# A two-layer perceiver kernel: input rows loaded alone, weight loads moved into the first chunks, the causal convolution's SiLU moved beside the x products

## What is computed

```
x = x + xattn0(layernorm(x), ctx, ctx)     # 8192 units: gelu(x @ ctx.T) @ ctx
x = x + mamba(layernorm(x), ...)           # W_in -> x_inner, z; causal conv of 4 taps;
                                           # silu; W_x; W_dt; selective scan; * silu(z); W_out
x = x + ffn0(layernorm(x), w1, w2)         # quantised weights and activations
x = x + xattn1(ctx, layernorm(x), ...)     # attention over 8192 + 512 keys
x = x + attn1(layernorm(x), ...)           # attention over channels
x = x + moe(layernorm(x), ...)             # 8 experts, top 2, and a shared one
```

## Time and profile before

| | |
|---|---|
| median of 3 runs | 2829.2 us (2828.49 to 2832.64) |
| the profiled execution, its own time | 2823.83 us |
| its span | 2822.1 us |
| TensorE matmul busy | 2561.9 us (91%) |
| VectorE busy | 1889.8 us (67%) |
| ScalarE busy | 1108.7 us (39%) |
| GpSimd busy | 529.2 us (19%) |
| mean granted TensorE clock | 0.954 of full |

### The profile page before, as it was taken

The page is one execution under the profiler, slowest core; times in us unless marked ns, Lnnn a source line. Parts: engine busy times, 40 slices in busy tenths (PEclk is TensorE's granted clock), DMA queues, the critical chain, the costliest instruction groups (busy, mean ns, idle before and its releaser), DMA issues.

```text
span 2822.1 us, 33960 instructions
## 1 busy us (share of the span) xinstructions
PE 2561.9 (91%) x11618; PEld 1674.2 (59%) x11618; DVE 1889.8 (67%) x2048; ACT 1108.7 (39%) x1340; POOL 529.2 (19%) x381
## 2 busy tenths in 40 slices
PE   6999988866755799999989999999989799999999
PEld 5778877622222566666654444444467677777775
DVE  5887853199988667777786666666545566666664
ACT  2333422333335322222215555555433355555553
POOL 4555542056630221111110000000010100000000
PEclk9999999999986899999989999999989899999999
DMA  7667745700010233343421232223111356666663
GB/s 281 234 237 253 259 132 164 268 8 15 23 60 1 94 134 146 124 173 119 163 90 61 90 124 100 90 90 125 40 45 45 123 206 223 225 225 223 224 224 131
DMA packets 105450, 394.40 MB, mean 140 GB/s; under 512 B 22842, under 2 KB 23046, under 8 KB 73108
## 3 DMA queue, kind: packets, MB, share of 16 engines
q1 hardware_dynamic: 77380, 326.61, 31.6%
q10 hardware_dynamic: 27984, 66.66, 6.7%
HBM read 303.93 MB, written 89.30 MB: 139 GB/s over the span
## 4 chain that ended last, share of the span: by engine, by line
PE 64%; DVE 11%; issue 3%; ACT 1%; POOL 1%; DMA 0%; DVEq 0%; SPq 0%; ACTq 0%; POOLq 0%
PE ps L1971 13%; PE ps L1973 12%; PE ps L1972 12%; PE ps L2269 10%; PE ps L2278 9%; DVE ps L1502 5%; PE ps L2209 3%; PE ps L2508 1%; DVE peak L1680 1%; PE ps L2119 1%; PE ps L2132 1%; DMA sh_raw<-in_s_parts 0%; DVE ln_st L1349 0%; DVE pre_conv L1569 0%; DVE read L1506 0%
## 5 line engine op out<-in xcount | busy, mean ns | idle before, releaser
L1723 DVE TENSOR_TENSOR sums<-sums,pT 128x1024 f32<-128x1024 f32 x272 | 333.3, 1225 | 199.9 <-ACT pT L1178 185.6
L1680 DVE SCALAR_TENSOR_TENSOR peak<-ps,rs_all,peak 128x1024 f32<-128x1024 f32 x272 | 348.7, 1282 | 120.2 <-PE ps L2209 107.5
L1178 ACT ACTIVATE pT<-ps,rs_all 128x1024 f32<-128x1024 f32 x272 | 288.2, 1111 | 239.5 <-DVE sums L1723 131.6
L2278 PE MATMUL ps<-pT,values 128*64 128x512 f32 x1088 | 263.4, 605 | 0.0
L2073 PE MATMUL ps<-read,ident 128*128 128x512 f32 x256 | 153.9, 703 | 85.7 <-DVE read L1506 85.7
L812 POOL TENSOR_TENSOR drive<-x_conv,bc_all 128x1024 f32<-128x1024 f32 x64 | 150.6, 2354 | 192.1 <-PE ps L1973 102.9
L1502 DVE TENSOR_TENSOR_SCAN ps<-ps,drive 128x512 f32<-128x512 f32 x128 | 156.2, 1220 | 2.2 <-ACT ps L1055 2.2
L2073 PEld LDWEIGHTS ps<-read,ident 128*128 128x128 f32 x256 | 43.1, 206 | 191.5 <-DVE read L1506 176.4
L848 POOL TENSOR_TENSOR cT_lo<-cT_raw,cT_hi 128x512 fp32r<-128x512 f32 x64 | 82.6, 1292 | 359.8 <-ACT cT_hi L1141 359.8
L1858 DVE TENSOR_TENSOR rgu_lo<-rgu_raw,rgu_hi 128x2048 fp32r<-128x2048 f32 x64 | 143.9, 2288 | 5.1 <-ACT rgu_hi L1261 5.1
L1055 ACT ACTIVATE ps<-delta,a_neg 128x512 f32<-128x512 f32 (+1 forms) x128 | 88.4, 691 | 149.2 <-DVE read L1506 149.2
(11 more groups left out here) (431 smaller groups left out, 6322.0 us busy)
## 6 DMA issues: line engine op xcount, KB each, us to landing
rgu_raw<-in_r_gate_up SPq DMA_DIRECT2D x64, 1024.0 KB, 4.8
rd_raw<-in_r_down SPq DMA_DIRECT2D x32, 1024.0 KB, 4.9
sh_raw<-in_s_parts SPq DMA_DIRECT2D x32, 768.0 KB, 4.2
key_rows<-key_hi SPq DMA_DIRECT2D x17, 1024.0 KB, 3.9
key_rows<-key_lo SPq DMA_DIRECT2D x17, 1024.0 KB, 5.9
value_rows<-values SPq DMA_DIRECT2D x17, 1024.0 KB, 8.9
ctxT_raw<-in_ctx_T SPq DMA_DIRECT2D x16, 1024.0 KB, 6.5
ctx_raw<-in_ctx SPq DMA_DIRECT2D x16, 1024.0 KB, 8.9
```

Of the source, the lines that this page charges most:

```text
L1178: nc.scalar.activation(pT[:, kt], ps[:, kt % 2 * 2:kt % 2 * 2 + 2], ACT.Exp, scale=rs_all[:, bass.ds(c * KT + kt, 1)]).then_inc(s4_exp.sem, 1)
L1680: nc.vector.scalar_tensor_tensor(peak[:, p], ps[:, kt % 2 * 2:kt % 2 * 2 + 2], rs_all[:, bass.ds(c * KT + kt, 1)], peak[:, p], ALU.mult, A ...
L1723: nc.vector.tensor_tensor(sums[:, p], sums[:, p], pT[:, kt], ALU.add).then_inc(s4_sum.sem, 1)
L2278: done = nc.tensor.matmul(ps[e * DK:(e + 1) * DK, 4 + p], values[:, s, kt, h * DK:(h + 1) * DK], pT[:, kt, e], start=start and kt == 0, st ...
```

## The change

Four edits. (1) SyncE waits for `x_res` to land before it issues the four first context loads. (2) The four loads of `w1` are no longer issued at the beginning but two each in `weight_work(0)` and `weight_work(1)`. (3) The four loads of `w2` are issued at n = 3 to 6 and not 1 to 4. (4) ScalarE applies the convolution's SiLU to block n - 2 directly behind the copy of x block n, from n = 2 on; the last two follow behind the gates of z blocks 1 and 2. The z gates are written out eight times and no longer in a loop. VectorE's, TensorE's and GpSimd's code is the same as before.

```diff
@@ block.sync
             sp.dma_start(x_res[:], a["x"].rearrange("o (t p) d -> p (o t) d", p=P)).then_inc(x_loaded, 16)
 
+            sp.wait_ge(x_loaded, 16)
             groups = a["ctx_1024"].rearrange("o (q s p j) d -> (o q) s p j d", s=2, p=P, j=GROUP)
@@ block.scalar
-            for c in range(W_CHUNKS):
-                load_weights(0, c)
             ln_evacuate(0)
@@ weight_work
-                if 1 <= n <= W_CHUNKS:
-                    load_weights(1, n - 1)
+                if n < 2:
+                    load_weights(0, 2 * n)
+                    load_weights(0, 2 * n + 1)
+                if 3 <= n < 3 + W_CHUNKS:
+                    load_weights(1, n - 3)
@@ x_turn and z_turn
                     nc.scalar.activation(x_in[:, n, TAPS - 1:], ps[:, 2 + k], ACT.Copy).then_inc(st_x.evac.sem, 1)
-
-            def z_turn(q, last):
-                for k in range(2):
-                    n = q * 2 + k
-                    act_e.wait_ge(*st_z.out(n + 1))
-                    nc.scalar.activation(gate[:, n], ps[:, 2 + k], ACT.Silu).then_inc(st_z.evac.sem, 1)
-                    act_e.wait_ge(conv_step, (n + 1) * TAPS)
-                    nc.scalar.activation(x_conv[:, n], ps[:, k], ACT.Silu).then_inc(conv_silu, 1)
+                    if not (isinstance(q, int) and q == 0):
+                        conv_out(n - 2, k)
+
+            def conv_out(n, k):
+                act_e.wait_ge(conv_step, (n + 1) * TAPS)
+                act_e.sem_inc(act_passed, 1)
+                nc.scalar.activation(x_conv[:, n], ps[:, k], ACT.Silu).then_inc(conv_silu, 1)
+
+            def gate_out(n):
+                act_e.wait_ge(*st_z.out(n + 1))
+                nc.scalar.activation(gate[:, n], ps[:, 2 + n % 2], ACT.Silu).then_inc(st_z.evac.sem, 1)
...
-            turns(act_e, IB // 2, z_turn)
+            for n in range(IB):
+                gate_out(n)
+                if 1 <= n < 3:
+                    conv_out(IB - 3 + n, (n - 1) % 2)
```

## The result

| | before | after |
|---|---|---|
| median of 5 runs each | 2832.64 us (2828.49 to 2836.24) | 2819.9 us (2814.86 to 2823.22) |
| profiled execution, its own time | 2823.83 us | 2821.91 us |
| its span | 2822.1 us | 2820.2 us |

The ratio is 0.9961 (95%: 0.9949 to 0.9973): faster by 0.39%, 11 us (8 to 14); the two medians alone lie 12.7 us apart. The forecast was 17.6 us. The direction was right. The time, 2819.9 us, lies above the forecast's own spread (2806 to 2817) and 0.1 us inside the range with the rivals (to 2820), and about a third of the forecast gain is missing. The two profiled executions differ by 2 us only: the one of before was faster than all five runs of the table, the one of after was the second slowest of its five. What a stage gained has to be read stage by stage, and in more than one execution.

The account below looks back on a forecast made before the run. TensorE was 64% of the span; the places changed were read from the timeline. 9.9 - 1.0 + (7.1 - 0.5) + 2.1 = 17.6 us gave 2806.2 us profiled, 2811.6 us median (-0.6%); spread 2806 to 2817, with rivals to 2820.

Parts of the forecast that it names:

- x in, first product: Front: x loaded alone lands at 6.3 us instead of 16.17, moving TensorE's first product 9.9 us earlier.
- w loads among the stores: Chunks: w loads sharing the units' queue meet stores at n = 4, 5, 6; cost 1.0 us, bounds 0 and 7.
- last x copy late: Projections: the copy of x block 7 waits for SiLU 4, so TensorE starts z 0.5 us late.
- hole before `xc_hi`: Projections: TensorE's 7.79 us wait after the z products shrinks to 0.69, a gain of 7.1 us.
- clock behind the hole: Projections: ten matmul steps run at full clock, 2.3 us instead of 4.40; gain 2.1 us, bounds 0 and 2.1.
- D: Rival, front: x is slow because it is first, landing no earlier than about 14 us; 2819.5 us, chance 0.05.
- B: Rival, front: context loads become the bound, costing 5 us; gain 12.6, 2816.6 us, chance 0.08.
- A: Rival, projections: x copies tied to the convolution, 3.54 us a block against 2.72; gain 12.8, 2816.4 us, chance 0.08.
- E: Rival, chunks: stores fall behind for good, holding every chunk from n = 3; slower, chance 0.02.
- that of 77.48: Chunks, earlier trace: `unit_hi` waited 2.70 us for a store at 77.48 us; TensorE lost 0.4 us and some more.
- C: Rival, chunks: the queue of units and w loads costs 7 us instead of 1; gain 11.6, 2817.6 us, chance 0.08.
- far bound: Projections: with a table load also in the turn after the loop, the last x copy is 1.8 us late.

Follow-up runs that it names:

- edit_1: The kernel before with only the context loads made to wait for x, w1's loads left at the beginning: 2832.72 us against 2831.73, ratio 1.0006.
- unrolled: The changed kernel with ScalarE's four x turns written out and no loop: 2816.77 us against 2831.73 for the kernel before, ratio 0.9939.
- after_again: The changed kernel, unchanged, profiled a second time: one execution of 2815.43 us.
- edits_1_to_3: The changed kernel with the x and z turns of the kernel before: 2823.59 us against 2827.14 for the kernel before, ratio 0.9986.
- small_late: The changed kernel with nine of 14 small parameter loads moved into the scan: 2809.76 us against 2831.91 for the kernel before, ratio 0.9927.
- before_again: The kernel before, unchanged, profiled a second time: one execution of 2828.48 us.
- edit_4: The kernel before with only the x and z turns of the changed kernel: 2820.21 us, ratio 0.9975 to the kernel before.
- w_on_sp: The changed kernel with all eight w loads on SyncE's queue behind the first four context loads: 2818.75 us against 2831.91 for the kernel before, ratio 0.9956.
- late_sp_unrolled: The changed kernel with nine small loads late, w loads on SyncE's queue and x turns written out: 2806.17 us, ratio 0.9915 to the kernel before.
- best: late_sp_unrolled with one more buffer each for `unit_raw`, `unit_lo` and `unit_hi`: 2799.75 us against 2831.91 for the kernel before, ratio 0.9892.

## Where the prediction went wrong, and what of it held

| step | forecast | measured | from |
|---|---|---|---|
| x in, first product | 9.9 | 9.6 | means 27.54 (four) and 17.97 (ten); 10.06 between before and after |
| w loads among the stores | -1.0 | -2.9 by chunk 12, -5.1 by the end | means below |
| last x copy late | -0.5 | -1.8 | wait before z 0.69 and 2.48 |
| hole before `xc_hi` | 7.1 | 7.1 | z to `xc_hi` 29.83 and 22.76 |
| clock behind the hole | 2.1 | 1.9 | next leg 8.36 and 6.42 |
| clock around the x stage | 0 | -1.4 | x to `xc_hi` 54.44 and 50.56, less the rows above |
| rest of the projections | 0 | 1.6 | x to scan 7.4 in all, 164.8 and 157.5 |
| sum | 17.6 | 11.9 | whole kernels: 11 (8 to 14) |

The projections' rows compare the four kernels with the old turns and the seven with the loop and edit 4.

**What held.** The mechanism of both gains. x was slow for its company (edit_1 has the same company on the other queue and the same 15.5 us), and not for being first, so D is out: alone it took 5.3 us, between the 5.0 us of the earlier trace rows and the 5.5 us of my sum. The context loads of B had their cover. The hole came out within 0.1 us, the low clock behind it within 0.2 us. A row decides on the drain that the Trainium skill (ScalarE: Activation LUTs, What ACT_TABLE_LOAD costs) adds to a table load, 1.38 us: in after the activations start 1.29 and 1.30 us behind the start of the 1.28 us loads, so the trace does not agree with 2.66 us each here. A, the copies tied to the convolution, is small: in unrolled the last copy stands behind a waiting SiLU, and the wait before z is 0.5 us longer than before. E did not come.

**The step that failed: "I expect one more wait like that of 77.48, about 1.0 us".** The term for the w loads was mis-sized: they cost 2.9 us by chunk 12 and about 5 us by the end of the block. With w2 at n = 3 to 6 the lateness at chunk 12 is 8.4, 8.1, 6.6 and 10.1 us (after, after_again, edits_1_to_3, unrolled), and 8.5 in small_late; with the old places it is 5.4, 5.6, 4.5 and 6.2 (before, before_again, edit_1, edit_4). The means of the first four and of the last four are 8.3 and 5.4, with no overlap. The three kernels that take the w loads off that queue have 5.9, 6.0 and 6.1: for the early loss the cause is shown. At the end the means are 24.1 and 19.0, 5.1 us, but the single values run from 16.7 to 30.6 and from 13.5 to 22.7, and about 1.1 us of the difference is that of the loss at chunk 60, which both kernels have. C named this mechanism and gave it 7 us; the truth lies between it and my value. The reason for the low value was that the waits in the earlier trace rows fell on time in which VectorE was busy. That held for waits of 1 to 2.7 us. The wait of 4.91 us in after left TensorE idle for 2.14 us, that of 9.74 us for 5.58 us, and a stall is followed by low clock (0.69 in unrolled, 0.56 in after behind the second). Whether the w loads also cost anything between chunk 12 and the end, beyond scatter, is open: w_on_sp is 25.4 us late at the end.

**The second step that failed: "SiLU 2 ends at 419.4 (with a table load, a new loop turn)".** I gave each loop turn one table load, before SiLU. There are two. TensorE's wait before z is 2.48 to 2.51 us in all seven kernels with the loop and 0.69 before: the last copy is 1.8 us late and not 0.5. That is the number of my far bound, but not its reason, since no table load comes behind the loop. unrolled, which differs in nothing else, waits 1.16 us, with one table load in all: so my 0.5 us is met there by a list with one load fewer than I had counted, which is luck.

I had put nothing down for the clock around this stage, and it cost 1.4 us more. In five of the seven kernels with the loop a stretch of low clock follows the late copy (z to `xc_hi` 24.34 to 24.39, not 22.76). In the other two, after_again and edit_4, there is none, but the stretch at the beginning of the x stage is longer, and x to z is 27.3 and 27.4. Windows of after, then of after_again: the beginning of the x stage, and the time from the first z product on.

```profile
403.90:408.00 4.10, 4.03 (x10) 3.16 (x11) 0.15 (x2) 0.00 (x0) 4.02 (x2) 0.50 0.00 0
430.40:436.00 5.60, 5.57 (x17) 4.45 (x18) 4.76 (x7) 1.19 (x2) 3.47 (x4) 0.70 0.10 34
```

```profile
398.89:404.90 6.01, 6.01 (x14) 4.75 (x15) 0.08 (x1) 0.48 (x1) 5.85 (x3) 0.50 0.00 0
426.30:436.00 9.70, 9.70 (x43) 8.04 (x44) 7.91 (x11) 3.20 (x6) 5.34 (x6) 1.00 0.39 121
```

The three kernels with the x turns written out have neither. The 1.6 us that the rest of the projections gave was not foreseen, and no run shows where it comes from; without it the sum would lie further off.

Two small slips do not matter: by their own terms SiLU 2 and SiLU 4 end at 419.1 and 424.9 and not at 419.4 and 425.1, and D's gain is 9.9 and not 9.7.

**The profile it was read from.** Before's execution lost nothing at chunk 60, before_again, edit_1 and edit_4 each 7 to 8 us. That does not touch the sum, since both kernels lose it, but it made the two profiled executions look alike and would have hidden the gain from whoever compares only them. Why that one escaped isn't known: there the long wait fell on the last unit, a chunk later, and was shorter, and TensorE lost 1 us by it. small_late shows that the nine small loads make the loss. How they hold up a store isn't shown; in after the DMA share was 0.34 and then 0.24 during it, so it is not a full DMA.

## What to carry to other kernels

Here the load that everything waited for became fast only when the other queue's loads were out of its way too, and not with its own queue empty. What is moved out of its way then has to be placed where no store with a shallow buffer is under way. Where an engine waits for a store before it may refill a buffer, look at what stands behind that wait in its list: here one more buffer for each of three tiles was worth 6.4 us (late_sp_unrolled to best), more than half of what the whole change brought. And take a second profile of the unchanged kernel before sizing small terms: here two differed by 7.7 us at one chunk.

## What the runs showed that I had not expected

- The 1 MB load of x in 2 KB runs took 5.3 us alone (after) and 15.5 us beside the other queue's four 1 MB loads in 8 KB runs, with nothing else on its own queue (edit_1).
- While the small parameter loads were in flight, a 256 KB store on the other queue took over 11 us, and the DMA engines were mostly idle. After, 356 to 368 us:

```profile
356.00:362.00 6.00, 6.00 (x28) 4.95 (x28) 3.72 (x7) 1.58 (x3) 2.96 (x2) 1.00 0.34 57
362.00:368.00 6.00, 3.49 (x16) 2.56 (x14) 0.00 (x0) 0.00 (x0) 0.00 (x0) 1.00 0.24 75
```

- In this hardware loop ScalarE had two table loads in each turn, before the first copy and before the first SiLU; in the same list written out (unrolled) one load served all copies and SiLUs that followed.
- The spread between executions, 8 us over five runs of before, is 0.9 us over four runs of best. Most of it went with the nine small loads (small_late: 2.5 us over five runs, with 82 us of waits on stores still there, against 5.6 us in w_on_sp beside it); the runs are few.
